# Per-image list positions, split load waits, a first mix on VectorE and an output bias made ahead of the experts

## What is computed

```python
h = concat([patches @ w.T + b, cls] + pos, txt)          # (32, 69, 256)
h = h + attn0(layernorm(h))      # 16 heads, causal, heads summed through one 16 x 256 WO
h = h + moe(layernorm(h))        # router argmax over 8 experts, 256 -> 512 -> 256, times its probability
h = h + attn1(layernorm(h))      # 16 heads, causal, c_proj 256 x 256
h = h + ffn(layernorm(h))        # 8-bit rows, ternary weights, 3-tap depthwise conv, silu, 256 -> 1024 -> 256
```

## Time and profile before

| | |
|---|---|
| three executions | 882.17, 888.98, 891.02 us |
| the profiled execution, its own time | 892.59 us |
| its span in the trace | 890.8 us |
| TensorE / VectorE / ScalarE / GpSimd busy | 86 / 67 / 50 / 43 % of the span |
| mean granted TensorE clock | 0.918 of full speed |
| layer 0 and router | 0 to 352 us |
| tables, weights | 352 to 373 us |
| experts | 373 to 481 us |
| first pairs of layer 1 fill | 481 to 560 us |
| layer 1 | 560 to 891 us |

### The profile page before, as it was taken

How to read it: one execution, slowest core, us unless ns; L and a number is a source line. 1 busy time by engine, 2 the same in 40 slices (tenths; PEclk the granted TensorE clock), 3 DMA queues, 4 the chain that set the end, 5 groups by cost and what they waited for, 6 DMA issues and landing times.

```text
span 890.8 us, 20394 instructions
## 1 busy us (share of the span) xinstructions
PE 766.9 (86%) x6953; PEld 675.2 (76%) x6953; DVE 597.1 (67%) x1444; ACT 441.7 (50%) x1048; POOL 382.3 (43%) x516
## 2 busy tenths in 40 slices
PE   2899899999999993299995699999999999999633
PEld 2799898899999882166764598888888888888432
DVE  0457576576767653622221246899999999999993
ACT  0344444344444442022221357677778777776551
POOL 0343445354546432222221666566666656553100
PEclk9999999899999995599998699899999999999755
DMA  5336420100000041122121000000000000000000
GB/s 166 105 89 278 121 56 8 21 11 15 9 8 8 8 155 44 18 58 68 54 72 37 12 10 9 7 15 14 15 15 15 17 17 15 15 9 7 13 7 13
DMA packets 23982, 36.41 MB, mean 41 GB/s; under 512 B 10037, under 2 KB 21210, under 8 KB 23114
## 3 DMA queue, kind: packets, MB, share of 16 engines
q1 hardware_dynamic: 14474, 26.20, 10.0%
q0 software_dynamic: 5808, 5.63, 3.0%
q10 hardware_dynamic: 3600, 3.28, 1.1%
HBM read 27.21 MB, written 7.88 MB: 39 GB/s over the span
## 4 chain that ended last, share of the span: by engine, by line
PE 47%; DVE 23%; issue 11%; DMA 10%; POOL 4%; ACT 3%; SPq 1%; DVEq 0%; POOLq 0%; ACTq 0%
DMA expert_lists<-token_no,slot_i 8%; PE bank_b L1427 5%; PE bank_h L1465 4%; PE bank_f L1439 3%; PE bank_e L1439 3%; PE bank_c L1476 3%; PE bank_e L1613 3%; DVE diff L898 3%; PE bank_g L1450 3%; PE bank_c L1629 3%; PE bank_a L1417 2%; PE bank_f L1613 2%; PE bank_d L1629 2%; PE bank_d L1465 2%; DVE w L1193 2%
## 5 line engine op out<-in xcount | busy, mean ns | idle before, releaser
L460 POOL TENSOR_TENSOR qbd<-qt,consts_f 128x560 f32<-128x560 f32 x128 | 163.5, 1284 | 181.0 <-PE bank_e L1439 99.3
L600 ACT ACTIVATE prob<-diff 112x345 f32<-112x345 f32 x128 | 62.1, 486 | 54.1 <-DVE diff L898 54.0
L606 ACT ACTIVATE pt<-bank_g 69x448 f32<-69x448 f32 x128 | 69.4, 542 | 32.4 <-PE bank_h L1450 31.0
L1450 PE MATMUL bank_g<-consts_f,prob 112*69 112x112 f32 x512 | 72.8, 265 | 9.0 <-ACT prob L600 9.0
L1465 PE MATMUL bank_h<-values,pt 69*69 69x68 f32 x1024 | 77.3, 230 | 2.2 <-ACT pt L615 2.2
L1465 PEld LDWEIGHTS bank_h<-values,pt 69*69 69x69 f32 x1024 | 72.6, 147 | 2.8 <-ACT pt L606 2.7
L1465 PEld LDWEIGHTS bank_d<-values,pt 69*69 69x69 f32 x1024 | 70.5, 143 | 2.2
L468 POOL TENSOR_TENSOR veps<-mv,consts_f 69x2 f32<-69x2 f32 x64 | 12.4, 194 | 139.1 <-DVE mv L913 98.9
L1439 PEld LDWEIGHTS bank_f<-kt,qbd 128*112 128x112 f32 x640 | 72.1, 180 | 0.0
L1439 PEld LDWEIGHTS bank_e<-kt,qbd 128*112 128x112 f32 x640 | 71.0, 178 | 1.4
L1465 PE MATMUL bank_d<-values,pt 69*69 69x68 f32 x1024 | 71.8, 226 | 0.0
(11 more groups left out here) (206 smaller groups left out, 1880.4 us busy)
## 6 DMA issues: line engine op xcount, KB each, us to landing
w<-in_w SPq DMA_DIRECT2D x2, 4096.0 KB, 14.4
patches<-in_patches SPq DMA_DIRECT2D x16, 222.0 KB, 2.6
expert_results<-prob ACTq DMA_DIRECT2D x25, 128.0 KB, 2.0
expert_rows<-x SPq DMA_DIRECT2D x16, 138.0 KB
out<-h SPq DMA_DIRECT2D x16, 138.0 KB
f_raw<-in_f SPq DMA_DIRECT2D x2, 1024.0 KB, 8.1
patches<-in_b SPq DMA_DIRECT2D x1, 2048.0 KB, 9.4
wqkv<-in_wqkv SPq DMA_DIRECT2D x2, 768.0 KB
```

The costliest lines, as they stand in the source:

```text
L460: pool.tensor_tensor(qbd[u % 2][:], q.broadcast_to([128, NG, HPB, QG]), head_mask.unsqueeze(1).unsqueeze(3).broadcast_to([128, NG, HPB, QG ...
L600: act.activation(prob[u % 2][:], diff[u % 2][:], ACT.Exp, scale=DH ** -0.5).then_inc(S["prob_made"], 1)
L606: act.activation(pt[u % 2][:, :, 0:4, :].rearrange("t h g q -> t g h q"), banks["g"][0:T, 0:4 * SR].rearrange("t (g h q) -> t g h q", g=4, ...
L1450: ins = nc.tensor.transpose(banks[bank][0:T, at * SR:(at + 1) * SR], prob[u % 2][:, g, :], ident[0:SR, 0:SR])
```

## The change

List places get a column for each image (`slot_i` is 69 x 32), so that VectorE's cast and GpSimd's transfers no longer wait for the pair before. Each stage waits only for the loads that it reads, the first loads are issued in another order (the embedding weights and the first two pairs of patches ahead of the rest), and ScalarE runs a one-element Exp at its start. The output bias of layer 1 is multiplied and added ahead of the experts, in bank `d` instead of `e`. GpSimd gathers without waiting for it, and for pair 0 the gate and the sum are two instructions of VectorE (`mix_first`) in place of two of ScalarE and one of GpSimd.

```diff
@@ -214,6 +214,7 @@
         zs = sb("zs", [T, 2, DH + 1])
+        table_probe = sb("table_probe", [1, 1])
         ot = sb("ot", [128, KC, 2, TP])
@@ -232,7 +233,7 @@
         slot = sb("slot", [T, B])
-        slot_i = sb("slot_i", [T, 2], I32)
+        slot_i = sb("slot_i", [T, B], I32)
@@ -282,6 +283,8 @@
         embed_w_in = sem("embed_w_in")
+        base_in = sem("base_in")
+        table_loaded = sem("table_loaded")
         patches_in = sem("patches_in")
@@ -350,21 +353,24 @@
         def _(sp):
+            def load_patches(n):
+                sp.dma_start(patch_v[:, bass.ds(n, 1), :, :], a["patches"][:, bass.ds(n, 1), :, :]).then_inc(patches_in, 16)
+
+            def load_text(n):
+                sp.dma_start(h[IMG:T, bass.ds(2 * n, 2), :],
+                             a["txt"][bass.ds(2 * n, 2)].rearrange("b t d -> t b d")).then_inc(text_in, 16)
+
+            sp.dma_start(w_tok[:, :, :], a["w_tok"]).then_inc(embed_w_in, 16)
+            load_patches(0)
+            load_patches(1)
             sp.dma_start(cf[:, :], a["consts_f32"]).then_inc(consts_in, 16)
+            sp.dma_start(base, a["pos"]).then_inc(base_in, 16)
+            sp.dma_start(tok_bias[0:1, :], a["cls"].unsqueeze(0)).then_inc(base_in, 16)
+            sp.dma_start(tok_bias[1:IMG, :], a["tok_b"].partition_broadcast(IMG - 1)).then_inc(base_in, 16)
             sp.dma_start(cb[:, :], a["consts_bf16"]).then_inc(consts_in, 16)
             sp.dma_start(token_no[:], a["token_no"]).then_inc(consts_in, 16)
-            sp.dma_start(w_tok[:, :, :], a["w_tok"]).then_inc(embed_w_in, 16)
-            sp.dma_start(base, a["pos"]).then_inc(embed_w_in, 16)
-            sp.dma_start(tok_bias[0:1, :], a["cls"].unsqueeze(0)).then_inc(embed_w_in, 16)
-            sp.dma_start(tok_bias[1:IMG, :], a["tok_b"].partition_broadcast(IMG - 1)).then_inc(embed_w_in, 16)
-
-            def load_pair(n):
-                sp.dma_start(patch_v[:, bass.ds(n, 1), :, :], a["patches"][:, bass.ds(n, 1), :, :]).then_inc(patches_in, 16)
-                sp.dma_start(h[IMG:T, bass.ds(2 * n, 2), :],
-                             a["txt"][bass.ds(2 * n, 2)].rearrange("b t d -> t b d")).then_inc(text_in, 16)
-
-            load_pair(0)
-            load_pair(1)
+            load_text(0)
+            load_text(1)
             for name, dst in (("wqkv0", wqkv), ("qk_bias", qk_bias)):
@@ -380,7 +386,8 @@
                 sp.wait_ge(text_in, 16 * n)
-                load_pair(n)
+                load_patches(n)
+                load_text(n)
@@ -448,7 +455,6 @@
             pool.wait_ge(consts_in, 48)
-            pool.wait_ge(zero_row_in, 32)
@@ -490,10 +496,11 @@
                 pool.wait_ge(slots_made, p + 1)
-                wait(pool, rows_listed, 32 * p)
+                if p == 0:
+                    pool.wait_ge(zero_row_in, 32)
                 for b in range(2):
                     pool.indirect_dma_start(
-                        lists, bass.IndirectOffsetOnAxis(slot_i[:, b:b + 1], 0), token_no[:, 2 * p + b:2 * p + b + 1], None,
+                        lists, bass.IndirectOffsetOnAxis(slot_i[:, 2 * p + b:2 * p + b + 1], 0), token_no[:, 2 * p + b:2 * p + b + 1], None,
                     ).then_inc(rows_listed, 16)
@@ -526,12 +533,10 @@
-            pool.wait_ge(attn1_w_in, 16 * 4)
+            pool.wait_ge(hid_made, TILES)
+            pool.memset(x2tb[:, :, :, T:TP], 0.0).then_inc(clears_done, 1)
             for k in range(2):
                 pool.wait_ge(y_stored[k], 16 * ((TILES - k + 1) // 2))
-            pool.wait_ge(hid_made, TILES)
-            pool.memset(x2tb[:, :, :, T:TP], 0.0).then_inc(clears_done, 1)
-            pool.wait_ge(o_bias_made, 1)
             S, BK, order = LS[1], BS[1], BANKS1
@@ -543,13 +548,17 @@
-                pool.wait_ge(y_gated, p + 1)
+                if p == 0:
+                    return
+                pool.wait_ge(y_gated, p)
                 hp = h[:, 2 * p:2 * p + 2, :]
...
                 pool.wait_ge(S["x_made"], 2 * p + 2)
+                if p == 0:
+                    pool.wait_ge(o_bias_made, 1)
                 hp = h[:, 2 * p:2 * p + 2, :]
@@ -580,7 +589,7 @@
             act.wait_ge(clears_done, 6)
-            act.wait_ge(attn0_w_in, 16 * 8)
+            act.activation(table_probe[:], zs[0:1, 0, DH:DH + 1], ACT.Exp).then_inc(table_loaded, 1)
@@ -630,6 +639,8 @@
                 wait(act, S["qbd_made"], UNITS * p)
+                if L == 0 and p == 0:
+                    act.wait_ge(attn0_w_in, 16 * 8)
                 for m in range(KC):
@@ -875,12 +888,9 @@
             S, BK, order = LS[0], BS[0], BANKS0
-            dve.wait_ge(consts_in, 48)
-            dve.wait_ge(clears_done, 6)
-            dve.wait_ge(embed_w_in, 16 * 4)
+            dve.wait_ge(base_in, 16 * 3)
             dve.tensor_tensor(base, base, tok_bias, ALU.add).then_inc(base_made, 1)
             dve.wait_ge(base_made, 1)
-            dve.wait_ge(attn0_w_in, 16 * 8)
@@ -950,7 +960,7 @@
-                dve.wait_ge(text_in, 16 * p + 16)
+                dve.wait_ge(text_in, max(32, 16 * p + 16))
                 dve.wait_ge(BK["b"], read_after(order, "b", "turn_e", p))
@@ -966,6 +976,9 @@
                 wait(dve, S["attended"], UNITS * p)
+                if p == 0:
+                    dve.wait_ge(attn0_w_in, 16 * 8)
+                    dve.wait_ge(clears_done, 6)
                 dve.tensor_tensor(
@@ -979,6 +992,8 @@
                 dve.wait_ge(logits_made, p + 1)
+                if p == 0:
+                    dve.wait_ge(consts_in, 48)
                 dve.tensor_tensor(lg[:], scored, br[:].unsqueeze(1).broadcast_to([T, 2, E]), ALU.add).then_inc(BK["a"], 1)
@@ -1002,8 +1017,7 @@
                                         onehot[:, bass.ds(2 * p + b, 1), :].rearrange("t b e -> t (b e)"), ALU.add))
-                wait(dve, rows_listed, 32 * p)
-                dve.tensor_copy(slot_i[:], slot[:, bass.ds(2 * p, 2)]).then_inc(slots_made, 1)
+                dve.tensor_copy(slot_i[:, bass.ds(2 * p, 2)], slot[:, bass.ds(2 * p, 2)]).then_inc(slots_made, 1)
                 c.end()
@@ -1099,6 +1113,9 @@
+            dve.wait_ge(attn1_w_in, 16 * 4)
+            dve.wait_ge(v_rows_projected, 1)
+            dve.tensor_tensor(o_bias1[:], banks["d"][0:T, 0:D], o_bias1[:], ALU.add).then_inc(o_bias_made, 1)
             dve.wait_ge(expert_w_in, 16 * 4)
@@ -1131,9 +1148,6 @@
-            dve.wait_ge(attn1_w_in, 16 * 4)
-            dve.wait_ge(v_rows_projected, 1)
-            dve.tensor_tensor(o_bias1[:], banks["e"][0:T, 0:D], o_bias1[:], ALU.add).then_inc(o_bias_made, 1)
             S, BK, order = LS[1], BS[1], BANKS1
@@ -1211,8 +1225,18 @@
+            def mix_first():
+
+                dve.wait_ge(y_gathered, 32)
+                dve.wait_ge(gates_made, 1)
+                for b in range(2):
+                    ins = dve.scalar_tensor_tensor(row_of(0, b), yg[:, b, :], gate[:, b:b + 1], row_of(0, b), ALU.mult, ALU.add)
+                ins.then_inc(h_mixed, 1)
+
             def stats1(p):
+                if p == 0:
+                    mix_first()
                 dve.wait_ge(h_mixed, p + 1)
@@ -1376,10 +1400,7 @@
             S, BK, order = LS[0], BS[0], BANKS0
-            pe.wait_ge(consts_in, 48)
-            pe.wait_ge(embed_w_in, 16 * 4)
-            pe.wait_ge(attn0_w_in, 16 * 8)
-            pe.wait_ge(clears_done, 6)
+            pe.wait_ge(embed_w_in, 16)
@@ -1404,12 +1425,19 @@
                 bank_is_free("c", "q", p)
+                first_weights(p)
                 query_or_key("c", 0).then_inc(S["q_made"], 1)
...
                 bank_is_free("a", "k", p)
+                first_weights(p)
                 query_or_key("a", 1).then_inc(S["k_made"], 1)
+
+            def first_weights(p):
+                if p == 0:
+                    pe.wait_ge(attn0_w_in, 16 * 8)
+                    pe.wait_ge(clears_done, 6)
@@ -1480,6 +1509,8 @@
                 bank_is_moved("c", "embed", p // 2 * 2 + 1)
+                if p == 0:
+                    pe.wait_ge(consts_in, 48)
                 bank_is_free("b", "turn_e", p)
@@ -1591,6 +1622,11 @@
+            pe.wait_ge(attn1_w_in, 16 * 4)
+            pe.wait_ge(v_rows_made, 1)
+            for c in range(KC):
+                ins = mm(banks["d"][0:T, 0:D], v_rows1[:, c, :], wo1[:, c, :], start=c == 0, stop=c == KC - 1)
+            ins.then_inc(v_rows_projected, 1)
             pe.wait_ge(expert_w_in, 16 * 4)
@@ -1625,6 +1661,8 @@
                 wait(pe, y_biased, t - 1)
+                if t == 1:
+                    pe.wait_ge(o_bias_made, 1)
                 for c in range(HC):
@@ -1657,10 +1695,6 @@
             pe.wait_ge(y_biased, TILES)
-            pe.wait_ge(v_rows_made, 1)
-            for c in range(KC):
-                ins = mm(banks["e"][0:T, 0:D], v_rows1[:, c, :], wo1[:, c, :], start=c == 0, stop=c == KC - 1)
-            ins.then_inc(v_rows_projected, 1)
...
```

## The result

The changed kernel took 856.96 us (median of four executions, 856.37 to 858.03) against 887.45 us (882.17 to 891.02): a ratio of 0.966, 95% interval 0.961 to 0.972. Forecast were 860 us and a range of 851 to 873. The profiled execution took 857.1 us with a span of 855.3, 35.5 less than the span of before; the sum had said 31.9. The profiled execution of before (892.59 us) was 5.1 us above its median, so between the medians the gain is 30.5 us.

The account below looks back on a forecast made before the run. The prediction took a chain of TensorE (47%), VectorE (23%) and transfers (10%), with VectorE's 37.3 us list wait, as the bound. 7.0 + 11.4 + 6.5 + 3.9 + 3.1 = 31.9 off 892.6 gave 860.7, forecast 860 us, range 851 to 873.

Parts of the forecast that it names:

- The steps of layer 0: Nine embedding steps, 88.17 to 264.17 us, fall to 18.29 us each without the list wait: 11.4 us, bounds 9 and 12.5.
- the three longest stalls: Lower bound for layer 0's steps: only these stalls come back, with nothing hidden elsewhere, 9 us.
- The fill-down: Behind layer 0's last embedding, 264 to 334 us: TensorE's idle time and half-rate clock return, 6.5 us, between 3.2 and 8.
- the last pair's serial tail: End of the stretch behind layer 0's last embedding, at half rate: if it gains too, that term becomes 8 us.
- The start: First matmul at 8.3 us instead of 14.72, table load hidden, 0.7 lost to late patches: 7.0 us, between 5.5 and 8.2.
- the start gives little: Rival at the start: the patches of pair 3 hold it, 3 us in place of 7, 864.7 us; chance 0.07.
- The last lists: Last cast 4.5 us earlier, last list transfers perhaps queued behind pair 14's: 3.9 us, between 2.4 and 4.5.
- The output bias: Its matmuls and addition move to where TensorE waits for the tables: costs nothing, 0.4 us without that cover.
- The turn: Turn to layer 1: gather 1.8 us earlier, two VectorE instructions save 1.3: 3.1 us, between 2.5 and 3.4.
- VectorE and GpSimd in each other's way: Rival in layer 0's steps: VectorE's small instructions stretch beside GpSimd, 1 us in each of 13 steps, 873.7 us; chance 0.08.
- GpSimd held by lists in flight: Rival in layer 0: GpSimd stands until earlier lists land, 5 us past slack in 14 steps, 931 us; chance 0.03.
- Layer 1 and the tail: Experts and layer 1 behind its first pair are untouched and move as blocks, distances within them unchanged.

Follow-up runs that it names:

- the lists alone: Kernel before with a list-place column for each image and no wait for the lists, nothing else: 868.87 us, ratio 0.982.
- the turn alone: Kernel before with only the output bias ahead of the experts, the gather not waiting for it and the first mix on VectorE: 883.37 us, ratio 0.996.
- The waits alone: Kernel before with each stage waiting only for the loads it reads, old load order, no early Exp: 882.87 us, ratio 0.996.
- the whole start: Kernel before with the new waits, load order and early Exp, old lists and old turn: 877.61 us, ratio 0.989.
- the mix put back: Changed kernel with pair 0's gate on ScalarE and sum on GpSimd again, bias and gather still early: 857.47 us, ratio 0.974.
- the longer series: Changed kernel with 28 and 55 idle TensorE matmuls ahead of the first tile and of layer 1: 854.85 us, ratio 0.970.
- all of these together: Changed kernel with early patches, idle matmuls before the first embedding, layer 1's wqkv loaded late, 28 and 55 idle matmuls in the pauses: 852.16 us, ratio 0.967.

## Why the prediction was right, step by step

**The steps of layer 0**: forecast 11.4 us, measured 20.9 - 9.5 = 11.4. The period is 18.29 us throughout, and the lists alone reproduce it. The agreement to a tenth belongs to this pair of traces: the waits, the start and the turn alone, which all keep the list wait, lose 14.4, 14.8 and 14.5 us in the same nine steps, though each ran shorter than the profiled kernel before. What carried the working is that the floor was read from the kernel itself, from a stretch in which the wait was short, and that of the 37.3 us of VectorE's wait only what passed the slack was counted. The lower bound of 9 was called the three longest stalls; the three longest steps alone are 10.6 over the floor (4.4, 4.9 and 1.4).

**The fill-down**: 6.5, measured 8.0 to `project` (28.9 - 20.9). The windows account for the 6.5: 3.2 us of idle time became 0.27, and the clock stayed at 1.00. The rest is the last pair's serial tail, which the working named as the way to 8 us: it ran at a mean clock of 0.53 (334 to 340 us before), and its first part runs at full speed now. One group shows it, first before, then after:

```profile
335.70 2.11 PE L1465 MATMUL bank_h<-values,pt 69*69 69x68 f32 x16 [0.87 <-ACT pt L615]
```

```profile
307.70 1.19 PE L1494 MATMUL bank_h<-values,pt 69*69 69x68 f32 x16 [0.87 <-ACT pt L624]
```

**The start**: 7.0, measured 9.5, outside its bounds of 5.5 to 8.2. This is the term that was mis-sized, in three places. The first matmul came at 6.24 and not at 8.3. I had taken the landing of `base` (9.20) as the measure of some 1.2 MB on the queue; with the change `base` lands at 9.00 while the embedding weights and two patch loads ahead of it, as many bytes, are in by 6.24. So the row held `base`'s own latency behind the bytes, and was no measure of them. The waits alone and the whole start put a number on the order of the loads: 10.85 and 6.24. The table load gave its 1.3 as forecast. By `queries` 2.0 were taken back (9.85 earlier at the second half of the first embedding, 7.84 there), not 0.7. The late patches of pair 3 are only the occasion: behind the wait for them the third embedding itself takes 3.33 us, with the granted clock at 0.50 from 17 to 21 us, where it took 1.68 before, and that is 1.65 of the 2.0. It takes 3.1 to 3.3 us in every kernel with this start and late patches. Then 1.65 us came back between `queries` and the fourth embedding, most of it from the clock, which no term had: the `values` group took 3.35 us before (31 to 34 us, granted clock 0.50) and 1.89 now. The 9.5 is also one pair of executions: the fourth embedding starts at 34.16 to 35.84 in three kernels with the old start and at 25.40 to 26.57 in seven with the new one, so 7.6 to 10.4. The rival "the start gives little" had the right obstacle and the wrong size.

**The last lists**: 3.9, measured 32.1 - 28.6 = 3.5 (`seen` stands at 351.49 and 322.85, 28.6 apart); 0.4 of it was lost again before the first tile. The cast's 4.57 us came back whole; the last transfer took 8.01 us and not 6.57, so the part that reached the tiles was smaller. In the nine other kernels without the list wait it took between 6.0 and 8.03 us. The bounds of 2.4 and 4.5 held.

**The output bias**: 0. As forecast. VectorE's addition at 338.86 ends 1.8 us ahead of the first tile's matmul at 341.08, which waits for its own gather.

**The turn**: 3.1, measured 34.8 - 31.7 = 3.1: the gather starts 0.29 us behind the landed store (2.20 before, so 1.9), the mix put back costs 1.37, and some 0.2 went again in the gather itself and the chain behind it. The Trainium skill ("GPSIMD Engine Reference", Key points) names contention with GpSimd for VectorE instructions with two inputs in SBUF, the on-chip memory, which these two have. GpSimd was idle beside them, so they do not test it: they took 479 ns each, 8 more than the 471 of the earlier trace rows.

**VectorE and GpSimd in each other's way.** The rival fell, and the small instructions became no longer. The group of four that finds a token's expert, by form over all pairs (busy us, mean ns), was 31.1 us before and is 23.3 now. The instruction just ahead of them, `lrel`, went the other way, from 5.7 to 10.2, so the five took 36.8 and take 33.5. It and the first of the four, after:

```profile
L1001 DVE TENSOR_TENSOR cand<-lg,lmax 69x16 f32<-69x16 f32 x16 | 15.2, 951 | 0.6
L1000 DVE TENSOR_TENSOR lrel<-lg,lmax 69x16 f32<-69x16 f32 x16 | 10.2, 636 | 0.5
```

Now of the four only the first is stretched, to 1062 ns at the median; before, any of three could be, up to 2247 ns. The lists alone have the new pattern too. That it is a matter of how the two engines' instructions fall beside each other is argued, not shown.

**GpSimd held by lists in flight.** It is not: no time ahead of its transfers is put down to a transfer, though the second transfer of a pair is issued 1.5 us behind the first, and a transfer takes at least 2.8 us to land.

**Layer 1 and the tail** were to keep their distances. They gained 0.7 us net (35.5 - 34.8). Behind that are +3.6 us in the fill (before ran 560 to 580 us at a mean clock of 0.83; after, no such window), -1.5 from the half-rate stretch at 472 to 480, and -1.6 from one late group of matmuls that took 3.60 us where it had taken 1.91. These stretches come and go between kernels that have the same layer 1. The time from the gather to the end was 405.6 us before, 403.7 after, 402.0 when the changed kernel ran again, and between 400.6 and 407.8 in the others. The clock falls there behind a wait of 1.23 us, in the changed kernel as with the longer series, but with all of these together it does not fall behind the same wait; what decides it stays open, and a term for a stretch at half rate has an uncertainty of some 3 us in this kernel.

**The three chips.** The kernel before differs by 12 us between the three chips, the changed one by 1 between the two on which it ran. That fits a wait on transfers as the part that varied, but no run measured the list wait on each chip, so it is argued only.

## What to carry to other kernels

A buffer that a transfer reads and an engine rewrites each step is a wait in the engine's own order, and costs what exceeds the slack of that step, plus the time at half rate behind each stall: read the floor from a step without the wait, and multiply by the steps. At a start, ask of each load what stands ahead of it in its queue, not only how many bytes; half of what the split waits could give came from the order. Filling a pause of TensorE with idle work gave nothing here when it ended 1.8 and 5.6 us early, and 1.3 us when it reached up to the next real work, where the next engine's latency took a part. Before an effect at the start is put down to an edit, look at the same group in kernels that have not got the edit: here the second embedding took 1.75 us in three of them.
